# Two of four SBUF-to-SBUF quarter copies moved to the SyncE queue, with the x and B-row loads placed behind their landing

## The chip, the cores and the metric

One Trainium2 chip; the kernel runs on one of its cores. The metric is device time in microseconds from the first to the last instruction of the program with what the runtime adds around it; three runs of the kernel before are given below. All traces are of one execution taken by the hardware profiler.

## What is computed

The reference has two layers over 128 sequences of 32 tokens with 512 features each:

```python
def lora_add(base, inp, A, B):                       # rank 16, one adapter per sequence, picked by index
    t = jnp.einsum('bri,bni->bnr', A[layer_idx][idx], inp)
    return base + jnp.einsum('bor,bnr->bno', B[layer_idx][idx], t) * 0.5
gate = lora_add(x @ W_gate.T, x, A_gate, B_gate)     # 512 -> 1376
up   = lora_add(x @ W_up.T,   x, A_up,   B_up)
act  = silu(gate) * up
down = lora_add(act @ W_down.T, act, A_down, B_down) # 1376 -> 512
x = x + down @ sign(weight).T + bias                 # layer 0
# layer 1: an adapter pair per sequence (64 adapters), then a 512x512 layer with 8 weighted LoRA terms
x = x + ffn(((x @ B1[idx1].T) @ A1[idx1].T))
```

The inputs are float32. The prologue folds the second matrices of both layers into tables, so that the loop has three kinds of products: gate and up (512 to 1376), down (1376 to 512, already multiplied with the signs), and the small adapter products.

## The kernel before

The 4096 tokens are worked through in `G = 32` groups of 128 tokens (four sequences). After a prologue of some 50 us each engine runs `step(g, prev, pp, ...)` for g = 0 to 31, the middle ones in a hardware loop, and then `finish`. The step is a software pipeline over three groups: gate and up of group `g`, down and the layer-0 adapter of group `prev = g - 1`, and layer 1 of group `pp = g - 2`.

The 1376 features are three chunks: chunk 0 of 352 columns, chunks 1 and 2 of 512. Float32 accuracy is had from high and low halves, three matmuls for each block. What the change touches is the way of chunk 2 of the activations from PSUM back to TensorE:

- TensorE ends a step with `second_rows`, which completes gate and up of chunks 1 and 2. In the next step ScalarE applies silu to chunk 1 and chunk 2, VectorE multiplies with up (`gated`) and transposes in 32x32 blocks (`turn_act`, signal `act_turned`: its count for chunk c of group g is `3 g + c + 1`).
- ScalarE then issues `send_act`: for each chunk four DMAs within SBUF, one for each quarter of 32 partitions of `act_sb[c]`, which is spread over the 128 partitions of `landed[c]`. Each of the four adds 16 to `act_in1` or `act_in2`. Before the change ScalarE issues four for chunk 1 and then four for chunk 2, and only then the casts of `split_actT`.
- TensorE meanwhile runs gate and up of chunk 0 and gate and most of up of chunk 1 of the new group. Before the last three matmuls of `up(g, 1)` stands `small_ready`: it waits for both chunks' landings (`act_in1`, `act_in2`), for the adapter rows `ad_in` and for the landed quarters and rows of layer 1. Behind it come the small adapter products (`t_rows`, `td_rows`, `t1_rows`, signal `small_mm`), `down` of chunks 1 and 0, and `first_ready`, which waits for `lhs_ready` (VectorE scales and transposes the small products), for the B rows (`b_in`) and for two more loads. Then `first_rows`, `down` of chunk 2, gate and up of chunk 2, and `second_rows`.
- SyncE issues all loads and stores of a step in one fixed order: x (`load_x`), four B rows (`load_b`), xT and four A rows for the next group (`load_xT` waits for `small_mm`), the copy of `lhs` (`copy_lhs`, waits for `lhs_ready`), four `b1` rows, the store (waits for `out_done`), four pairs of `ad` and `sb` rows, four `c` rows. Where a row is picked by an index, SyncE first loads the index into a register. `load_x` waits before the change for the transpose of chunk 1 (`act_turned` at `3 g + 2`); this also keeps `load_b` from overwriting `b_rows` while `second_rows` reads it.

Lines: `send` L240, `send_act` L245, `load_b` L297, `load_xT` L331, `load_x` L336, `store` L343, `copy_lhs` L347, SyncE's `step` L351, ScalarE's `step` L463, `turn_small` L613, `gate` L794, `up` L807, `down` L819, `small_ready` L864, `first_ready` L893, `first_rows` L901, `second_rows` L913, TensorE's `step` L923. All matmuls of gate and up have line L785.

Of the kernel before, what the change touches and what calls it, by code (L numbers as in the profile page):

```python
# [8 lines left out]
BATCH, SEQ, H = 128, 32, 512  # L9
# [15 lines left out]
NC = len(CHUNKS)  # L25

QUAD = P // 4
SENT = 4 * 16
TURN_W = [3 * P, 4 * P, 4 * P]
# [47 lines left out]
def build_adaln_ffn(nc, xT, x, wgu, signT, wd, bd, btab, atab, adtab, la, lbw, w1T, a1, b1tab, b1end,  # L77
                    bias, ids, consts, sb_table, c_table, out):
    ctx = ExitStack()
    with ctx:  # L80
# [4 lines left out]
        def place(name, shape, dtype, at=None, line=LINE):  # L85
            n = 4 * int(np.prod(shape[1:]))
            n = (n + line - 1) // line * line
            if at is None:
                at = cursor
            t = nc.alloc_sbuf_tensor_at(name, shape, dtype, offset=at[0])  # L90
            at[0] += n
            return t
# [23 lines left out]
        x1_turn = place("x1_turn", [P, H], f32)  # L116
        act_sb = [place(f"act_sb{c}", [P, w], f32) for c, w in enumerate(TURN_W)]
        landed = [place(f"landed{c}", [P, w], f32) for c, w in enumerate(TURN_W)]
        x1_landed = place("x1_landed", [P, H], f32)
# [55 lines left out]
        def sem(name):  # L175
            return ctx.enter_context(nc.semaphore(name))
# [19 lines left out]
        L = {n: sem(n) for n in names}  # L196
# [12 lines left out]
        def last(g):  # L209

            return isinstance(g, int) and g == G - 1
# [12 lines left out]
        def act_in(c):  # L224

            return L[("act_in0", "act_in1", "act_in2")[c]]
# [10 lines left out]

            return slice(b * SEQ, (b + 1) * SEQ)

        def send(engine, to, tile, w, signal):  # L240
            for q in range(4):
                engine.dma_start(to[:, q * w // 4:(q + 1) * w // 4], tile[q * QUAD:(q + 1) * QUAD, 0:w]  # L242
                                 ).then_inc(signal, 16)

        def send_act(engine, g, c):  # L245
            engine.wait_ge(L["act_turned"], g * NC + c + 1)
            send(engine, landed[c], act_sb[c], TURN_W[c], act_in(c))

        def send_x1(engine, g):
            engine.wait_ge(L["x1_turned"], g + 1)  # L250
            send(engine, x1_landed, x1_turn, H, L["x1T_in"])

        def rows_stored(engine):

# [5 lines left out]
        def _(sp):  # L260
# [31 lines left out]
            def load_a(g):  # L292
                for b in range(GB):
                    at = row_of(0, g, b, R0)
                    sp.dma_start(a_raw[:, b, :], atab[bass.ds(at, P), :]).then_inc(L["a_in"], 16)

            def load_b(g):  # L297
                for b in range(GB):
                    at = row_of(0, g, b, R0)
                    sp.dma_start(b_rows[even_rows(0, 4), b, :],  # L300
                                 btab[bass.ds(at, P), :].rearrange("(q r e) w -> q r (e w)", q=4, e=2)
                                 ).then_inc(L["b_in"], 16)

            def load_b1(g):
                for b in range(GB):
                    at = row_of(1, g, b, R1)
                    sp.dma_start(b1_raw[:, b, :], b1tab[bass.ds(at, P), :]).then_inc(L["b1_in"], 16)

            def load_ad_sbd(g):
                if isinstance(g, int) and g < 2:  # L310
                    sp.wait_ge(L["first_mm"], g + 1)
                for b in range(GB):
                    at = row_of(0, g, b, R0)
                    sp.dma_start(ad_raw[:, b, :], adtab[bass.ds(at, P), :]).then_inc(L["ad_in"], 16)
                    sp.dma_start(cs_rows[even_rows(3, 4), b, :], sb_view[bass.ds(at, P), :].rearrange("(r e) w -> r (e w)", e=8)
                                 ).then_inc(L["sbd_in"], 16)

            def load_c(g):
                if last(g):
                    sp.wait_ge(L["first_mm"], g + 2)  # L320
                for b in range(GB):
                    at = row_of(1, g, b, R1)
                    sp.dma_start(cs_rows[even_rows(2, 3), b, :], c_view[bass.ds(at, P), :].rearrange("(r e) w -> r (e w)", e=8)
                                 ).then_inc(L["c_in"], 16)
# [6 lines left out]
            def load_xT(g):  # L331
                after(sp, L["small_mm"], g)
                sp.dma_start(xT_raw[:], xT[bass.ds(g * P, P), :].rearrange("p (k t) -> p k t", k=KC)
                             ).then_inc(L["xT_in"], 16)

            def load_x(g):  # L336
                if last(g):
                    sp.wait_ge(L["x1_done"], g)
                else:
                    sp.wait_ge(L["act_turned"], g * NC + 2)  # L340
                sp.dma_start(x_in[:], x[bass.ds(g * P, P), :]).then_inc(L["x_in"], 16)

            def store(g):  # L343
                sp.wait_ge(L["out_done"], g + 1)
                sp.dma_start(out[bass.ds(g * P, P), :], out_sb[:]).then_inc(L["stored"], 16)

            def copy_lhs(g):  # L347
                sp.wait_ge(L["lhs_ready"], g + 1)
                sp.dma_start(lhs2_sb[2 * QUAD:P, :], lhs_sb[0:2 * QUAD, :]).then_inc(L["lhs2_in"], 16)

            def step(g, prev, pp, nxt):  # L351
                if prev is not None:
                    load_x(prev)
                    load_b(g)
                if nxt is not None:
                    load_xT(nxt)
                    load_a(nxt)
                copy_lhs(g)
                if prev is not None:
                    load_b1(prev)  # L360
                if pp is not None:
                    store(pp)
                load_ad_sbd(g)
                if prev is not None:
                    load_c(prev)

            def finish(g):
                load_x(g)
                sp.wait_ge(L["small_mm"], g + 2)
                for b in range(GB):  # L370
                    at = row_of(1, g, b, R1)
                    sp.dma_start(b1_raw[:, b, :], b1end[bass.ds(at, P), :]).then_inc(L["b1_in"], 16)
                load_c(g)
                store(g - 1)
                sp.wait_ge(L["out_done"], g + 1)
                sp.dma_start(out[g * P:(g + 1) * P, :], x1_turn[:]).then_inc(L["stored"], 16)
                sp.wait_ge(L["stored"], 16 * G)

            sp.wait_ge(S["rows_clear"], 1)
            load_b(0)  # L380
            sp.wait_ge(S["rows_clear"], 2)
            step(0, None, None, 1)
            step(1, 0, None, 2)
            step(2, 1, 0, 3)
            with sp.Fori(3, G - 1) as g:
                step(g, g - 1, g - 2, g + 1)
# [41 lines left out]
        def _(act):  # L428
# [3 lines left out]
            def split_xT(g):  # L432
                act.wait_ge(L["xT_in"], 16 * g + 16)
                for half in range(2):
                    after(act, L["xT_used"], 2 * g - 1 + half)
                    at = slice(2 * half, 2 * half + 2)
                    copy(xT_sb[:, at, 0, :], xT_raw[:, at, :]).then_inc(L["xT_hi"], 1)

            def silu(g, c):
                w = CHUNKS[c][1]  # L440
                act.wait_ge(L["first_mm" if c == 0 else "second_mm"], g + 1)
                after(act, act_in(c), SENT * g)
                nc.scalar.activation(act_sb[c][:, 0:w], gu_ps[GU_BANK[c][0]][:, 0:w], ACT.Silu  # L443
                                     ).then_inc(L["silu_done"], 1)
# [6 lines left out]
            def split_actT(g, c):  # L451
                act.wait_ge(act_in(c), SENT * g + SENT)
                high_actT(c)

            def split_up(c, pieces):

                f, w = CHUNKS[c]
                act.wait_ge(S["down_mm"], BLOCKS_UNTIL[c])
                for k in pieces:
                    act.wait_ge(wu_in[k], 16)  # L460
                    copy(wu_sb[:, 0, k, f:f + w], wu_raw[:, k, f:f + w]).then_inc(S["wu_hi"], 1)

            def step(g, prev, pp, nxt):  # L463
                if prev is not None:
                    silu(prev, 1)
                    silu(prev, 2)
                    send_act(act, prev, 1)
                    send_act(act, prev, 2)
                    split_actT(prev, 1)
                    split_actT(prev, 2)  # L470
                else:
                    split_up(2, range(KC))
                silu(g, 0)
                send_act(act, g, 0)
                if prev is not None:
                    send_x1(act, prev)
                split_actT(g, 0)
                if nxt is not None:
                    split_xT(nxt)
# [663 lines left out]
```

## Time and profile before

| what | us |
|---|---|
| median of three runs | 1050.86 (1047.32 to 1051.44) |
| the profiled execution, its own time | 1048.76 |
| its span, first to last instruction | 1046.4 |
| TensorE matmul busy | 958.4 (92%) |
| TensorE weight load busy | 737.9 (71%) |
| VectorE busy | 430.2 (41%) |
| ScalarE busy | 170.5 (16%) |
| GpSimd busy | 93.5 (9%) |
| mean granted TensorE clock | 0.949 of full |

The profile counts as busy only compute; instructions that issue DMAs are shown as queues (SPq, ACTq), with the time that the engine spends on the issue. The time "to landing" of a DMA runs from the start of its issue to its completion. An idle time with the word "issue" behind it is one for which the profile shows no releaser. The chain of waits is followed back from the last instruction.

### The profile page before, as it was taken

What the parts mean: (1) busy time and instruction counts of PE and PEld (TensorE: products, weight loads), DVE (VectorE), ACT (ScalarE), POOL (GpSimd) and SP (SyncE); (2) the same over time, 40 slices, a digit from 0 to 9 for tenths busy, and PEclk for the clock granted to TensorE, in tenths of its full rate; (3) what the DMA queues carried; (4) which work ended last, traced back from release to release, by engine and by line L of the source; (5) the groups of instructions that cost most, each with busy time, mean ns of one, the idle gap of its engine ahead of it and who ended that gap; (6) DMA issues with size and microseconds to landing.
All of it is one profiled execution on the core that took longest, in us unless ns stands there. A gap on an engine that the chain in (4) does not pass through costs nothing.

```text
span 1046.4 us, 28196 instructions
## 1 busy us (share of the span) xinstructions
PE 958.4 (92%) x10528; PEld 737.9 (71%) x10528; DVE 430.2 (41%) x1051; ACT 170.5 (16%) x318; POOL 93.5 (9%) x81
## 2 busy tenths in 40 slices
PE   9999989999888889988898988898998988899888
PEld 6877767677666767766676766767676667677665
DVE  6753344344333334434343443433444343344433
ACT  6731011111101111110111111111111011111101
POOL 0200000000000000000000000000000000000001
PEclk9999899999999999999999999999999999999989
DMA  9824444453444444344454434444534434453432
GB/s 352 350 69 119 120 115 135 124 138 95 123 122 112 132 128 122 105 129 113 120 132 129 112 108 131 114 123 122 139 107 110 131 107 132 121 139 102 117 94 74
DMA packets 166678, 135.23 MB, mean 129 GB/s; under 512 B 55680, under 2 KB 138368, under 8 KB 166528
## 3 DMA queue, kind: packets, MB, share of 16 engines
q1 hardware_dynamic: 93712, 101.08, 33.5%
q10 hardware_dynamic: 72000, 30.70, 11.1%
q0 software_dynamic: 944, 3.15, 0.8%
q8 instruction: 14, 0.23, 0.1%
q14 instruction: 8, 0.07, 0.0%
HBM read 92.11 MB, written 11.01 MB: 99 GB/s over the span
## 4 chain that ended last, share of the span: by engine, by line
PE 89%; issue 8%; DMA 1%; DVE 1%; ACTq 1%; ACT 0%; SPq 0%
PE gu_ps L785 48%; PE y_ps L829 26%; PE out_ps L849 3%; PE gu_ps L918 3%; PE out_ps L886 2%; PE out_ps L838 2%; PE out_ps L859 1%; PE y_ps L785 1%; PE out_ps L785 1%; PE gu_ps L909 1%; ACTq L242 1%; DMA weff_raw<-in_w1T 1%; DMA landed<-act_sb 0%; PE gu_ps L958 0%; PE y_ps L890 0%
## 5 line engine op out<-in xcount | busy, mean ns | idle before, releaser
L785 PE MATMUL gu_ps<-wu_sb,xT_sb 128*128 128x512 f32 (+1 forms) x1152 | 265.1, 375 | 80.1 <-issue 79.1
L785 PEld LDWEIGHTS gu_ps<-wu_sb,xT_sb 128*128 128x128 f32 x1152 | 205.6, 189 | 120.9 <-issue 93.0
L829 PE MATMUL y_ps<-down_sb,actT_sb 128*128 128x512 f32 x1056 | 273.8, 413 | 0.0
L785 PE MATMUL gu_ps<-wg_sb,xT_sb 128*128 128x512 f32 (+1 forms) x1152 | 255.7, 371 | 0.6 <-DVE xT_sb L576 0.6
L829 PEld LDWEIGHTS y_ps<-down_sb,actT_sb 128*128 128x128 f32 x1056 | 204.8, 200 | 69.6 <-issue 27.3
L785 PEld LDWEIGHTS gu_ps<-wg_sb,xT_sb 128*128 128x128 f32 x1152 | 204.2, 188 | 55.7 <-DVE xT_sb L576 26.7
L576 DVE TENSOR_TENSOR actT_sb<-landed,actT_sb 128x512 fp32r<-128x512 f32 (+1 forms) x96 | 69.9, 728 | 260.4 <-ACT actT_sb L430 259.4
L430 ACT CAST actT_sb<-landed 128x512 fp32r<-128x512 f32 (+1 forms) x96 | 56.3, 586 | 492.1 <-issue 280.3
L596 DVE TENSOR_TENSOR act_sb<-act_sb,gu_ps 128x512 f32<-128x512 f32 (+1 forms) x94 | 58.2, 619 | 122.5 <-ACT act_sb L443 122.5
L619 DVE STREAM_TRANSPOSE lhs_sb<-t_own 32x32 f32<-32x32 f32 x512 | 103.7, 203 | 7.7
L443 ACT ACTIVATE act_sb<-gu_ps 128x512 f32<-128x512 f32 (+1 forms) x96 | 49.8, 553 | 339.4 <-PE gu_ps L909 310.7
L399 POOL TENSOR_TENSOR x_sb<-x_sb,bias_sb 128x512 f32<-128x512 f32 x31 | 39.8, 1284 | 527.4 <-DVE x_turn L632 527.4
L610 DVE TENSOR_TENSOR t_own<-out_ps,const_sb 128x64 f32<-128x64 f32 (+3 forms) x34 | 7.5, 222 | 169.0 <-PE out_ps L859 163.5
L395 POOL TENSOR_TENSOR x_in<-x_in,bias_sb 128x512 f32<-128x512 f32 x32 | 41.3, 1290 | 366.5 <-DMA x_in<-in_x 366.5
L600 DVE STREAM_TRANSPOSE act_sb<-act_sb 128x512 f32<-128x512 f32 (+1 forms) x94 | 62.7, 667 | 3.2
L849 PE MATMUL out_ps<-ad_raw,landed 128*32 128x16 f32 x2816 | 42.2, 211 | 0.0
L849 PEld LDWEIGHTS out_ps<-ad_raw,landed 128*32 128x32 f32 x2816 | 40.1, 151 | 0.2 <-issue 0.2
L918 PE MATMUL gu_ps<-b_rows,lhs_sb 32*32 32x512 f32 x1024 | 36.6, 601 | 0.0
L890 PE MATMUL y_ps<-cs_rows,lhs_sb 32*32 32x512 f32 x256 | 35.8, 600 | 0.0
L886 PE MATMUL out_ps<-cs_rows,lhs_sb 32*32 32x512 f32 x256 | 35.8, 600 | 0.0
L576 DVE TENSOR_TENSOR xT_sb<-xT_raw,xT_sb 128x256 fp32r<-128x256 f32 x64 | 26.7, 422 | 3.4 <-ACT xT_sb L430 0.6
L627 DVE TENSOR_TENSOR x_sb<-x_in,y_ps 128x512 f32<-128x512 f32 x31 | 21.3, 688 | 16.1 <-PE y_ps L829 16.1
(135 smaller groups left out, 441.3 us busy)
## 6 DMA issues: line engine op xcount, KB each, us to landing
b_rows<-in_btab SPq DMA_DIRECT2D x128, 216.0 KB, 3.5
landed<-act_sb ACTq DMA_DIRECT2D x248, 64.0 KB, 2.8
ad_raw<-in_adtab SPq DMA_DIRECT2D x128, 88.0 KB, 2.1
xT_raw<-in_xT SPq DMA_DIRECT2D x32, 256.0 KB, 2.6
a_raw<-in_atab SPq DMA_DIRECT2D x128, 64.0 KB, 1.8
x_in<-in_x SPq DMA_DIRECT2D x32, 256.0 KB, 2.9
x_landed<-x_turn ACTq DMA_DIRECT2D x124, 64.0 KB, 2.3
out_x<-out_sb SPq DMA_DIRECT2D x31, 256.0 KB, 2.1
```

Source lines behind the costliest of these rows:

```text
L395: nc.gpsimd.tensor_tensor(x_in[:], x_in[:], bias_sb[:, 0, :], ALU.add).then_inc(L["x_biased"], 1)
L430: return nc.scalar.copy(o, i)
L443: nc.scalar.activation(act_sb[c][:, 0:w], gu_ps[GU_BANK[c][0]][:, 0:w], ACT.Silu).then_inc(L["silu_done"], 1)
L576: return nc.vector.tensor_tensor(o, whole, hi(high), ALU.subtract)
L596: nc.vector.tensor_tensor(a, a, gu_ps[GU_BANK[c][1]][:, 0:w], ALU.mult).then_inc(L["act_done"], 1)
L600: nc.vector.transpose(act_sb[c][:], act_sb[c][:]).then_inc(L["act_turned"], 1)
L619: turned = nc.vector.transpose(lhs_sb[r * QUAD:(r + 1) * QUAD, tokens(b)], wide[tokens(b), :])
L785: last = nc.tensor.matmul(o, w, m, start=start and n == 0, stop=stop and n == len(terms) - 1, skip_group_check=not check)
L829: last = nc.tensor.matmul(y_ps[:], actT_sb[:, ACTT_SLOT[c] + n, a, :], down_sb[:, blk, b, :], start=c == begin and n == 0 and (a, b) == (0 ...
L849: last = nc.tensor.matmul(small_ps[tokens(b), TD_AT:TD_AT + TD_W], landed[c][:, at:at + SEQ], ad_raw[:, b, blk * RANK:(blk + 1) * RANK], s ...
L886: return nc.tensor.matmul(out_ps[tokens(b), :], lhs_sb[group(2), tokens(b)], cs_rows[group(2), b, :], start=True, stop=True, skip_group_ch ...
L918: last = nc.tensor.matmul(gu_ps[GU_BANK[c][u]][tokens(b), :], lhs[group(r), tokens(b)], b_rows[group(r), b, CHUNKS[0][1]:PAIR], start=Fals ...
```

## The change

SyncE's step issues quarters 0 and 1 of chunk 2 of group `prev`, after the transpose of that chunk; ScalarE issues quarters 2 and 3. `load_x`, and with it everything behind it on SyncE, waits for the landing of all four quarters of chunk 2 instead of the transpose of chunk 1.

```diff
-        def send(engine, to, tile, w, signal):
-            for q in range(4):
+        def send(engine, to, tile, w, signal, quarters):
+            for q in quarters:
                 engine.dma_start(to[:, q * w // 4:(q + 1) * w // 4], tile[q * QUAD:(q + 1) * QUAD, 0:w]
                                  ).then_inc(signal, 16)
 
-        def send_act(engine, g, c):
+        def send_act(engine, g, c, quarters=range(4)):
             engine.wait_ge(L["act_turned"], g * NC + c + 1)
-            send(engine, landed[c], act_sb[c], TURN_W[c], act_in(c))
+            send(engine, landed[c], act_sb[c], TURN_W[c], act_in(c), quarters)
...
@@ load_x (SyncE)
                 if last(g):
                     sp.wait_ge(L["x1_done"], g)
                 else:
-                    sp.wait_ge(L["act_turned"], g * NC + 2)
+                    sp.wait_ge(L["act_in2"], SENT * (g + 1))
                 sp.dma_start(x_in[:], x[bass.ds(g * P, P), :]).then_inc(L["x_in"], 16)
...
@@ step (SyncE)
                 if prev is not None:
+                    send_act(sp, prev, 2, range(0, 2))
                     load_x(prev)
                     load_b(g)
...
@@ step (ScalarE)
                     send_act(act, prev, 1)
-                    send_act(act, prev, 2)
+                    send_act(act, prev, 2, range(2, 4))
                     split_actT(prev, 1)
                     split_actT(prev, 2)
```

## Rows read from the trace of the kernel before

**Rows 1.** The page: shares of the longest chain, and the costliest matmul group with its idle time.
```profile
PE 89%; issue 8%; DMA 1%; DVE 1%; ACTq 1%; ACT 0%; SPq 0%
L785 PE MATMUL gu_ps<-wu_sb,xT_sb 128*128 128x512 f32 (+1 forms) x1152 | 265.1, 375 | 80.1 <-issue 79.1
```
**Rows 2.** Waits (engine, line, releaser: us in total, times, longest): TensorE's at 80 to 90 us, then SyncE's at 170 to 990 us.
```profile
PE gu_ps L785 <- DMA landed<-act_sb: 1.0, 1, 1.0
...
SPq L333 <- PE out_ps L859: 142.1, 27, 6.4
SPq L345 <- DVE out_sb L644: 10.6, 20, 1.0
```
**Rows 3.** Timeline of TensorE (start, duration, what, idle before): first, second, middle and last stall.
```profile
112.86 0.95 PE L785 MATMUL gu_ps<-wu_sb,xT_sb 128*128 128x512 f32 x3 [2.10 <-issue]
...
145.44 0.96 PE L785 MATMUL gu_ps<-wu_sb,xT_sb 128*128 128x512 f32 x3 [2.66 <-issue]
...
531.01 1.14 PE L918 MATMUL gu_ps<-b_rows,lhs_sb 32*32 32x512 f32 x32
...
543.01 1.06 PE L785 MATMUL gu_ps<-wu_sb,xT_sb 128*128 128x512 f32 x3 [2.03 <-issue]
...
1003.22 0.93 PE L785 MATMUL gu_ps<-wu_sb,xT_sb 128*128 128x512 f32 x3 [2.51 <-issue]
```
**Rows 4.** Windows: length, busy of PE, PEld, DVE, ACT, POOL; granted clock, DMA share, GB/s.
```profile
84.30:86.30 2.00, 1.94 (x123) 1.57 (x123) 0.00 (x0) 0.46 (x1) 0.00 (x0) 1.00 0.00 0
...
145.44:147.83 2.39, 2.37 (x155) 1.89 (x156) 0.00 (x0) 0.26 (x1) 0.00 (x0) 1.00 0.03 7
147.83:152.80 4.97, 4.97 (x27) 3.87 (x29) 4.16 (x18) 0.00 (x0) 0.00 (x0) 1.00 0.34 94
152.80:172.20 19.40, 19.36 (x146) 14.84 (x145) 7.13 (x13) 3.41 (x7) 1.55 (x2) 1.00 0.47 122
540.98:543.01 2.03, 0.00 (x1) 0.01 (x1) 0.90 (x1) 0.37 (x1) 0.35 (x1) 1.00 0.98 298
543.01:546.20 3.19, 3.19 (x156) 2.64 (x156) 0.00 (x0) 0.26 (x1) 0.00 (x0) 0.61 0.14 54
546.20:551.58 5.38, 5.38 (x25) 4.17 (x21) 4.16 (x18) 0.00 (x0) 0.00 (x0) 0.91 0.36 98
551.58:570.99 19.41, 19.41 (x146) 14.86 (x145) 7.44 (x13) 3.41 (x7) 2.57 (x2) 1.00 0.49 127
```
**Rows 5.** Timeline of VectorE and ScalarE: last transpose, all eight sends, the fifth on, the last.
```profile
535.10 0.71 DVE L600 STREAM_TRANSPOSE act_sb<-act_sb 128x512 f32<-128x512 f32 x1
...
534.52 5.39 ACTq L242 DMA_DIRECT2D landed<-act_sb  x8
...
537.22 1.21 ACTq L242 DMA_DIRECT2D landed<-act_sb  x2
537.79 1.46 ACTq L242 DMA_DIRECT2D landed<-act_sb  x2
...
539.28 0.62 ACTq L242 DMA_DIRECT2D landed<-act_sb  x1
```
**Rows 6.** DMA issues, us to landing: sends starting 536.42, 538.45 and 539.28, each alone.
```profile
landed<-act_sb ACTq DMA_DIRECT2D x1, 64.0 KB, 2.2
landed<-act_sb ACTq DMA_DIRECT2D x1, 64.0 KB, 3.9
landed<-act_sb ACTq DMA_DIRECT2D x1, 64.0 KB, 3.3
```
**Rows 7.** Timeline of SyncE's queue from one xT load to the next; last B row apart.
```profile
516.90 0.34 SPq L333 DMA_DIRECT2D xT_raw<-in_xT  x1
517.95 3.06 SPq L295 DMA_DIRECT2D a_raw<-in_atab  x4
521.06 0.52 SPq L349 DMA_DIRECT2D lhs_sb<-lhs_sb  x1
...
536.87 0.33 SPq L341 DMA_DIRECT2D x_in<-in_x  x1
537.78 3.88 SPq L300 DMA_DIRECT2D b_rows<-in_btab  x4
546.47 0.34 SPq L333 DMA_DIRECT2D xT_raw<-in_xT  x1
...
541.19 0.47 SPq L300 DMA_DIRECT2D b_rows<-in_btab  x1
```
**Rows 8.** One tile's DMAs, us from issue to landing, min, median, max: landed, then b_rows (500 to 562 us).
```profile
DMA to landing us min/median/max: 2.0/2.5/4.0
...
DMA to landing us min/median/max: 3.0/3.4/3.7
```

More of the change, by code:

```diff
@@ L238, in tokens @@
             return slice(b * SEQ, (b + 1) * SEQ)
-        def send(engine, to, tile, w, signal):
-            for q in range(4):
+        def send(engine, to, tile, w, signal, quarters):
+            for q in quarters:
                 engine.dma_start(to[:, q * w // 4:(q + 1) * w // 4], tile[q * QUAD:(q + 1) * QUAD, 0:w]
                                  ).then_inc(signal, 16)
-        def send_act(engine, g, c):
+        def send_act(engine, g, c, quarters=range(4)):
             engine.wait_ge(L["act_turned"], g * NC + c + 1)
-            send(engine, landed[c], act_sb[c], TURN_W[c], act_in(c))
+            send(engine, landed[c], act_sb[c], TURN_W[c], act_in(c), quarters)
         def send_x1(engine, g):
             engine.wait_ge(L["x1_turned"], g + 1)
-            send(engine, x1_landed, x1_turn, H, L["x1T_in"])
+            send(engine, x1_landed, x1_turn, H, L["x1T_in"], range(4))
         def rows_stored(engine):
```

## Prediction

> **What bounds the kernel now.** I read the page first: TensorE holds 89% of the chain that ended last and "issue" another 8%; nearly all of the latter is one place, 79.1 us of idle time before matmuls of gate and up, L785 [rows 1]. The reader is to see that this is no spread-out loss. The timeline of TensorE shows it as one stall in each step, always before the three matmuls that stand behind `small_ready`: thirty stalls of 2.0 to 3.3 us, from 112.86 to 1003.22, and a shorter one of 1.0 us in step 1 [rows 2, 3]. So 29 periods fill 1003.22 - 112.86 = 890.4 us, 30.70 us each. What `small_ready` waits for is told by ScalarE's queue: eight sends take 5.39 us from 534.52 on, the last starts at 539.28 and lands 3.3 us later, at 542.6; TensorE goes on at 543.01 [rows 3, 5, 6]. The fourth send (536.42) landed in 2.2 us, before SyncE's x load (536.87) and B rows were on the way, the seventh and eighth needed 3.9 and 3.3 us [rows 6, 7], with the DMA engines at 0.98 of their time in the stall [rows 4]. The change goes at both halves of this delay: the queueing on ScalarE and the shared DMA engines.
>
> The stall has a second cost. Behind it TensorE's granted clock drops from 1.00, that is 2.4 GHz, to half, 1.2 GHz, for a stretch: 0.61 and 0.91 in the two windows after 543.01. In step 3 the clock stayed at 1.00 although the stall was 2.66 us; from the three matmuls to `first_rows` that took 2.39 + 4.97 = 7.4 us, against 3.19 + 5.38 = 8.6 with the drop [rows 4]. The remaining 19.4 us of a step are the same in both. So TensorE's own work is 26.7 us a step at full clock, 28.0 with the drop: 30.70 is 28.0 and a stall of 2.7.
>
> **The change part by part.** Let T be the end of `second_rows`, 531.01 + 1.14 = 532.15 in the step shown [rows 3]. TensorE reaches `small_ready` at T + 8.8 (540.98).
>
> *ScalarE's sends.* It now issues six instead of eight. The sixth started at 537.79, T + 5.6, instead of the eighth at T + 7.1 [rows 5]. Nothing else of its own is moved; its cast of chunk 1 comes up to 1.4 us earlier, which no one waits for.
>
> *The landing of chunk 2.* With x and B rows held back, a quarter should land in 2.2 us (the fourth send's value, which I take, since it too had only other sends beside it); bounds 2.0 and 4.0 from all sends [rows 6, 8]. ScalarE's half is there at T + 7.8, 1.0 before TensorE asks. It costs nothing up to a landing of 3.2.
>
> *SyncE's own circle.* This is the dear part. From xT (516.90) to x (536.87) SyncE needs 19.97 us of issuing; from x to the end of the fourth B row (541.66) 4.79; and from there to xT at least 0.05 (the gap behind the A rows before `copy_lhs`, the nearest row) [rows 7]. That is 24.8 us of work, and the rest of the period is its wait for `small_mm` at xT, 142.1 us in 27 steps, 5.3 each [rows 2]. The change adds, before x: two sends, the second 0.65 after the first (eight in 5.39 us), its landing 2.2, and waking up with the register work for x, 0.15, an estimate that lies below the 0.4 TensorE took from the landing (542.6) to 543.01. That is 3.0, so SyncE can't go round in under 27.8 us. Bounds: 0.57 + 2.0 gives 27.4 (and 27.2 if the B rows issue faster without ScalarE's beside them); 0.83 (538.45 to 539.28) + 3.3 + 0.4 gives 29.3 [rows 6]. Its wait of 5.3 us is what pays for this, and it goes nearly whole. In this state SyncE comes to the sends later than the transpose (535.81, T + 3.7), so that the wait for the transpose costs nothing, and TensorE may wait some tenths for SyncE's half.
>
> *The B rows.* They now start behind the landing. x at T + 8.0, the fourth B row 4.32 later (541.19 - 536.87), landed after 3.0 to 3.4 [rows 7, 8], at T + 15.3 to 15.7. TensorE wants them before the last three matmuls of `down(prev, 0)`: after 8.8 + 7.4 - 0.8, T + 15.4 at full clock, T + 16.6 with the drop. From there to the next T it needs some 11.6 us (three matmuls 0.75, `first_rows` to `second_rows` 10.6, and 0.3 to start again). This circle thus lasts 26.9 to 27.3, up to 28.4 with the slowest landings. The rows had more than a microsecond of cover before, and now have none at full clock.
>
> *What moves with it.* xT, the A rows, the copy of `lhs`, the `b1` rows, the store, the `ad` and `sb` rows and the `c` rows all stand behind the wait. In the new period xT is issued some 1.5 us later against TensorE than now; all of them are wanted in the next step, or, as the copy of `lhs`, 8 us after its issue. The x load is wanted only by GpSimd and by VectorE's sum after `down(prev, 2)`, 12 us on. I cost them at nothing.
>
> A rule that speaks against the half of the change that shares the sends: the Trainium skill, "DMA: Bandwidth & Descriptors", sections "Issuing engines are not separate DMA queues" and "Rules for kernel authors", says that DMAs from several engines run on the same 16 DMA engines and that this saves only issue time. The rows agree that sharing the engines costs landing time (2.2 against 3.9). By the rule the split would be worth just the two sends' issue, T + 7.1 to T + 5.6. The gate alone would then give a landing at T + 9.3, a stall of 0.5 to 0.8 and a period near 28.5, an estimate; with the split the sum stays as worked out here.
>
> **The sum.** The period is the largest of three: TensorE 26.7 or 28.0, SyncE 27.8, B rows 27. If the clock stays up, SyncE sets 27.8 and TensorE stalls 1.1 us a step; if it still drops, TensorE sets 28.0 nearly without a stall. In step 1, with a stall of 1.0, it stayed at 1.00 [rows 2, 4]. Both ends lie so near that I take 28.0. Then 29 x (30.70 - 28.0) = 78.3, and about 2 more from the stalls of step 1 and 2 (1.0 and 2.1, half of each kept): 80. The tail is untouched: step 31 has no xT and no A rows to issue, and the last x load waits for `x1_done` as before. The profiled execution's 1048.8 becomes 968.5; the median of the runs lies 2.1 above that execution, so 970.
>
> **Rivals.**
>
> 1. *Forecast*, period 27.7 to 28.4: 958 to 979. Chance 0.52.
> 2. *SyncE's circle is longer* than I count, because sends from two engines at once issue in 0.83 and land in 3.3, or the B rows are late in addition: period 28.4 to 29.3, 980 to 1006. For it: 24.8 of the 27.8 are measured, but the 3.0 comes from ScalarE's rows. Chance 0.24.
> 3. *The circles overlap better*: the clock stays full and both circles fall to 27.2: 29 x 3.5 + 3 = 104, 946; up to 957. Against it: it needs the lower bounds all at once. Chance 0.17.
> 4. *Slower.* The B rows take the stall's place at `first_ready`. With the slowest landings, sends 4.0 and B rows about 4.2 by estimate (0.8 over the median), the circle is 5.6 + 4.0 + 0.15 + 4.3 + 4.2 + 11.6 = 29.9; the clock would then drop in dense matmuls, 3.4 us at half speed (two windows: 0.39 of 3.19 and 0.09 of 5.38 us lost, doubled), costing up to 1.7: 31.6, 29 x 0.9 = 26 us slower, 1077. It decides from a period over 30.7, a circle without clock loss of over 29. Against it: the sends land alone. Chance 0.04.
> 5. *The change does not do what it says*: SyncE comes so late to its two quarters that they land no earlier than the eighth send did (T + 10.4). It would need SyncE free only at T + 7.6; before it was free at 536.87, T + 4.7. Time 1050. Chance 0.03.
>
> **How the numbers follow.** 970 is the forecast of case 1. The range takes cases 1 and most of 2 and 3: 950 to 1002. A change below 0.5% (5 us) can't be told from none here. Faster by over 0.5% is cases 1 to 3 and a little of the next: 0.93; within 0.5%: 0.03; slower 0.04.
>
> **What would show it.** Right: the idle time before L785 falls from 79 to under 35 us; SyncE's wait for `small_mm` at L333 falls from 5.3 to about nothing in a step and a wait for the landing of about 2 us stands before x; the sends land in about 2.2; the xT loads follow each other at 27.8 to 28.2 us. Wrong: xT loads at over 29 us or under 27.5; a stall before L829 or L886 that is larger than the old one; a landing of over 3 us of sends that nothing accompanies. Should the clock still drop in every step with no stall before it, TensorE's 28.0 was the bound and not SyncE.

## The result and the profile after

| | before | after |
|---|---|---|
| median, us | 1051.15 | 962.34 (960.8 to 964.34) |
| ratio to before | | 0.9167, 95% interval 0.9135 to 0.92 |
| span of the profiled execution | 1046.4 | 959.9 |
| mean granted TensorE clock | 0.949 | 0.998 |

The change makes the kernel 8.3% faster. The median before is of four runs, one of them a slow outlier of 1488.36 us; without it the median is 1050.86, and the ratio leaves it out. The first line below is the page's chain by engine, the others its costliest groups with idle time (line, engine, what, count, then busy, mean ns of one, then idle before it). Lines below `send_act` have moved down by one: gate and up are L786, down is L830.

```profile
PE 95%; issue 3%; DMA 1%; DVE 0%; ACT 0%; ACTq 0%; SPq 0%
...
L830 PE MATMUL y_ps<-down_sb,actT_sb 128*128 128x512 f32 x1056 | 267.1, 401 | 13.8 <-issue 13.7
L786 PE MATMUL gu_ps<-wu_sb,xT_sb 128*128 128x512 f32 (+1 forms) x1152 | 256.6, 369 | 7.1 <-issue 7.1
```

The idle time at gate and up went from 80 us to 7 [rows 1]; 14 us of a new idle time stand before down. The stall has become small and has in part moved from `small_ready` to `first_ready`. The waits of SyncE's queue at 170 to 900 us (line, releaser: us in total, times, longest) tell what it waits for now:

```profile
SPq L341 <- DMA landed<-act_sb: 37.0, 26, 1.5
```

That is the only one. The wait for `small_mm` at xT, 5.3 us in each step before [rows 2], is gone, and so is that for the store; SyncE now waits 1.4 us in each step for the landing, and for nothing else. Its own timeline, from xT load to xT load (start, duration, what), to be laid beside [rows 7]:

```profile
504.58 0.34 SPq L333 DMA_DIRECT2D xT_raw<-in_xT  x1
...
524.16 1.37 SPq L242 DMA_DIRECT2D landed<-act_sb  x2
527.23 0.34 SPq L341 DMA_DIRECT2D x_in<-in_x  x1
528.15 3.77 SPq L300 DMA_DIRECT2D b_rows<-in_btab  x4
532.30 0.34 SPq L333 DMA_DIRECT2D xT_raw<-in_xT  x1
```

This is a closed circle of 27.72 us: 19.58 from xT to the first send, 3.07 from there over the landing to x, 4.69 to the end of the B rows, 0.38 to xT. The 26 xT periods from 171.6 to 893.2 us have a mean of 27.76. TensorE in the same step shows what it has left over. The first row is the three matmuls behind `small_ready`, as in [rows 3]; the other two are `down` of chunks 1 and 0, cut by the wait for the B rows before its last three matmuls:

```profile
527.42 0.96 PE L786 MATMUL gu_ps<-wu_sb,xT_sb 128*128 128x512 f32 x3 [0.27 <-issue]
...
529.89 4.36 PE L830 MATMUL y_ps<-down_sb,actT_sb 128*128 128x512 f32 x18
534.86 0.94 PE L830 MATMUL y_ps<-down_sb,actT_sb 128*128 128x512 f32 x3 [0.61 <-issue]
```

These are two stalls, of 0.27 and 0.61 us. The windows over this step (columns as in [rows 4]) are at full clock throughout:

```profile
527.42:529.89 2.47, 2.47 (x156) 2.02 (x156) 0.00 (x0) 0.26 (x1) 0.00 (x0) 1.00 0.49 140
529.89:535.73 5.84, 5.23 (x25) 3.75 (x22) 4.17 (x18) 0.00 (x0) 1.29 (x1) 1.00 0.68 204
535.73:555.10 19.37, 19.37 (x147) 15.01 (x147) 7.76 (x13) 3.89 (x8) 1.28 (x1) 1.00 0.42 112
```

The quarters of all three chunks land in 1.9, 2.2 and 3.2 us (min, median, max at 170 to 900 us), against 2.0, 2.4 and 4.6 before. These figures hide most of the effect, since they count the quarters of chunks 0 and 1 in. The four quarters of chunk 2 alone, over the same time, went from a median of 3.6 us to 2.2, and their last landing from T + 11.1 to T + 8.6, in the mean of the steps. T is the end of `second_rows`, as in the prediction.

### The profile page after: what moved, and what is told of

Its sections match the earlier page's. It is cut to its first block, busy times and chain, and to the rows that moved or that the text cites. A ratio compares the mean times of both kernels' runs of the same rounds, so it can differ in the third digit from the quotient of the medians.

```text
span 959.9 us, 28224 instructions
## 1 busy us (share of the span) xinstructions
PE 928.4 (97%) x10528; PEld 708.2 (74%) x10528; DVE 422.8 (44%) x1051; ACT 170.2 (18%) x318; POOL 93.2 (10%) x81
## 4 chain that ended last, share of the span: by engine, by line
PE 95%; issue 3%; DMA 1%; DVE 0%; ACT 0%; ACTq 0%; SPq 0%
PE gu_ps L786 52%; PE y_ps L830 27%; PE gu_ps L919 3%; PE out_ps L850 3%; PE out_ps L887 2%; PE y_ps L786 1%; PE out_ps L839 1%; PE out_ps L786 1%; PE gu_ps L910 1%; PE out_ps L860 1%; PE gu_ps L959 0%; DMA landed<-act_sb 0%; DMA lb_raw<-in_lbw 0%; PE gu_ps L1031 0%; ACTq L242 0%
## 5 line engine op out<-in xcount | busy, mean ns | idle before, releaser
L830 PE MATMUL y_ps<-down_sb,actT_sb 128*128 128x512 f32 x1056 | 267.1, 401 | 13.8 <-issue 13.7
L786 PE MATMUL gu_ps<-wu_sb,xT_sb 128*128 128x512 f32 (+1 forms) x1152 | 256.6, 369 | 7.1 <-issue 7.1
L830 PEld LDWEIGHTS y_ps<-down_sb,actT_sb 128*128 128x128 f32 x1056 | 192.0, 189 | 89.8 <-issue 39.8
L786 PE MATMUL gu_ps<-wg_sb,xT_sb 128*128 128x512 f32 (+1 forms) x1152 | 256.0, 371 | 1.5 <-DVE xT_sb L577 1.5
L786 PEld LDWEIGHTS gu_ps<-wg_sb,xT_sb 128*128 128x128 f32 x1152 | 204.3, 188 | 56.9 <-DVE xT_sb L577 27.8
L786 PEld LDWEIGHTS gu_ps<-wu_sb,xT_sb 128*128 128x128 f32 x1152 | 204.7, 188 | 44.0 <-issue 16.1
L577 DVE TENSOR_TENSOR actT_sb<-landed,actT_sb 128x512 fp32r<-128x512 f32 (+1 forms) x96 | 62.2, 648 | 221.9 <-ACT actT_sb L431 220.9
L850 PE MATMUL out_ps<-ad_raw,landed 128*32 128x16 f32 x2816 | 34.1, 186 | 0.0
L850 PEld LDWEIGHTS out_ps<-ad_raw,landed 128*32 128x32 f32 x2816 | 31.5, 108 | 0.5 <-issue 0.2
L577 DVE TENSOR_TENSOR xT_sb<-xT_raw,xT_sb 128x256 fp32r<-128x256 f32 x64 | 26.6, 421 | 4.6 <-ACT xT_sb L431 3.8
```

The source lines that it names most:

```text
L577: return nc.vector.tensor_tensor(o, whole, hi(high), ALU.subtract)
L786: last = nc.tensor.matmul(o, w, m, start=start and n == 0, stop=stop and n == len(terms) - 1, skip_group_check=not check)
L830: last = nc.tensor.matmul(y_ps[:], actT_sb[:, ACTT_SLOT[c] + n, a, :], down_sb[:, blk, b, :], start=c == begin and n == 0 and (a, b) == (0 ...
L850: last = nc.tensor.matmul(small_ps[tokens(b), TD_AT:TD_AT + TD_W], landed[c][:, at:at + SEQ], ad_raw[:, b, blk * RANK:(blk + 1) * RANK], s ...
```

## The experiments

Three theories are tested:

- Theory A: in the changed kernel SyncE's own circle of issues sets the period, not TensorE and not the B rows' landing.
- Theory B: the sharing of the sends carries the gain and the place of the loads does little.
- Theory C: the place of the loads behind the landing (the gate, below) carries it.

All edits are made to the changed kernel. The ratio is that to the kernel before, timed on the same chip; the period from xT to xT is the mean at 170 to 900 us of one trace.

| kernel | median us | ratio, 95% interval | us from xT to xT |
|---|---|---|---|
| changed | 962.3 | 0.9167 (0.9135 to 0.92) | 27.76 |
| loads behind the landing, sends not shared | 983.7 | 0.9393 (0.9334 to 0.9452) | 28.40 |
| sends shared, loads not behind the landing | 939.5 | 0.8957 (0.8902 to 0.9012) | 26.81 |
| neither, x behind the transpose of chunk 2 | 1049.2 | 0.999 (0.9973 to 1.0008) | 30.29 |
| changed, one more issue on SyncE | 981.3 | 0.9352 (0.9294 to 0.941) | 28.42 |
| changed, four more issues | 1024.6 | 0.9772 (0.973 to 0.9814) | 29.81 |
| changed, B rows before x | 959.7 | 0.9149 (0.9092 to 0.9205) | 27.77 |
| changed, x issued by GpSimd | 946.0 | 0.8998 (0.8963 to 0.9033) | 27.26 |
| changed, x before the landing | 944.8 | 0.8993 (0.8961 to 0.9025) | 27.19 |
| sends shared, B rows not behind the landing, x by GpSimd | 927.3 | 0.8833 (0.8801 to 0.8866) | 26.59 |

### Each half of the change alone

```diff
@@ gate only: SyncE's step
-                    send_act(sp, prev, 2, range(0, 2))
@@ ScalarE's step
-                    send_act(act, prev, 2, range(2, 4))
+                    send_act(act, prev, 2)
```

> The changed kernel, but ScalarE sends all four quarters of chunk 2 (x and the B rows stay behind their landing). Theory A (SyncE's circle of issues bounds the changed kernel, 27.7 us a step): here SyncE has two sends less, its circle is no bound; the eighth send leaves at T + 7.1 and lands alone at T + 9.3, so TensorE stalls 0.5 to 0.8 us at small_ready, the B rows come 1.4 us later, and the period is 28.0 to 28.5: 970 to 985 us. Theory B (the sharing of the sends carries the gain, the place of the loads little): stall of 2 us or more and the clock drop stay, over 1020. Theory C (the gate alone carries it): 962, as the changed kernel.

Measured: 983.7 us, period 28.40. Rows of TensorE, ScalarE and SyncE's x load (start, duration, what), with the end of `second_rows` at 528.42 + 1.15 = 529.57 as T:

```profile
528.42 1.15 PE L918 MATMUL gu_ps<-b_rows,lhs_sb 32*32 32x512 f32 x32
...
539.26 0.96 PE L785 MATMUL gu_ps<-wu_sb,xT_sb 128*128 128x512 f32 x3 [0.86 <-issue]
...
531.93 5.43 ACTq L242 DMA_DIRECT2D landed<-act_sb  x8
...
538.90 0.62 ACT L430 CAST actT_sb<-landed 128x512 fp32r<-128x512 f32 x1 [0.82 <-DMA landed<-act_sb]
...
539.07 0.33 SPq L341 DMA_DIRECT2D x_in<-in_x  x1
```

The cast starts at the landing, T + 9.3, as theory A had it; TensorE has stalled 0.86 here, and 0.7 in the mean (17.4 us in 26 stalls). It waits almost as much for the B rows before `down`, 16.0 us in 26. Theories B and C are out as stated: the gate alone gives three quarters of the changed kernel's gain (65 of 89 us, each against the kernel before on its own chip), and the rest needs the sharing.

```diff
@@ split only: load_x
-                    sp.wait_ge(L["act_in2"], SENT * (g + 1))
+                    sp.wait_ge(L["act_turned"], g * NC + 3)
```

> The changed kernel, but x waits only for the transpose of chunk 2, not for the landing; the sends stay shared. Theory A: SyncE's circle loses the 2.4 us between its second send and x, to about 25.5 of issue, and waits for small_mm again; the loads run beside ScalarE's last two sends, which then land in 3 to 3.9 instead of 2.2, at T + 8.6 to 9.5, a stall of 0 to 0.8 us: period 26.9 to 27.6, 940 to 960 us. Theory C (without the gate the contention brings the stall back): stall of 1.5 to 2.5 and the clock drop again, 985 to 1030. If landing is what counts and SyncE's circle nothing: slower than the changed kernel by the added stall.

Measured: 939.5 us, period 26.81, just under the range of theory A, and faster than the changed kernel by more than either interval. SyncE's queue, and what ScalarE waits for:

```profile
514.47 1.34 SPq L242 DMA_DIRECT2D landed<-act_sb  x2
516.02 0.44 SPq L341 DMA_DIRECT2D x_in<-in_x  x1
517.05 3.79 SPq L300 DMA_DIRECT2D b_rows<-in_btab  x4
...
512.33 3.85 ACTq L242 DMA_DIRECT2D landed<-act_sb  x6
...
518.64 0.62 ACT L431 CAST actT_sb<-landed 128x512 fp32r<-128x512 f32 x1 [1.61 <-DMA landed<-act_sb]
```

From its first send to x SyncE needs 1.55 us instead of 3.07. It waits for `small_mm` again (12.1 us in 23 waits), so its circle is no bound. And the contention that the gate should keep away is small: both queues' sends have left by 516.2, just as x starts, and the last has landed by 518.64. It isn't nothing: the last quarter of chunk 2 lands in 2.9 us here (median at 170 to 900 us), against 2.2 in the changed kernel and 4.1 before. Once the sends are shared, the loads leave behind them by the order on the queue alone. In the kernel before, x and the B rows left beside the fifth to the eighth send [rows 5, 7].

So the sharing does two things at once. In the mean of the steps the last send leaves at T + 5.6 instead of T + 7.1, and x at T + 6.1 instead of T + 4.7. The last landing of chunk 2 comes 2.75 us earlier than before (T + 8.37 against T + 11.12): 1.45 of it is the earlier send, the rest the shorter landing. No run has one of these without the other. The two halves of the change are then two remedies for one stall, and beside the sharing the gate costs more than it brings: it lengthens SyncE's circle.

The control for this run: it also moves x from behind the transpose of chunk 1 to that of chunk 2.

```diff
-                    sp.wait_ge(L["act_in2"], SENT * (g + 1))
+                    sp.wait_ge(L["act_turned"], g * NC + 3)
-                    send_act(sp, prev, 2, range(0, 2))
-                    send_act(act, prev, 2, range(2, 4))
+                    send_act(act, prev, 2)
```

> A control: the kernel before, with x waiting for the transpose of chunk 2 instead of chunk 1; ScalarE sends all eight quarters. Theory A: SyncE reached x at T + 4.7 already, behind that transpose at T + 3.7, so nothing changes: within 4 us of the kernel before, the stall of 2.7 us and the clock drop stay. It shows whether the later signal alone, without the sharing, explains the run in which only the sends were shared. Rival (x and B rows starting a little later let the eighth send land sooner): 5 to 20 us faster.

Measured: 1049.2 us, ratio 0.999. The later signal does nothing by itself; x leaves at T + 4.7 as before. The period of 30.29 is from one of the two quickest of its twelve runs, 1041.4 us.

### Is SyncE's circle the bound?

```diff
@@ SyncE's step
                 load_ad_sbd(g)
                 if prev is not None:
+                    after(sp, L["spare_in"], 16 * prev)
+                    sp.dma_start(spare[:], consts[:, 0:16]).then_inc(L["spare_in"], 16)
                     load_c(prev)
```

> The changed kernel with one more small load (8 KB, needed by nobody) on SyncE in each step, ahead of the c rows. Theory A: SyncE's circle is the bound, so each step grows by the whole issue, 0.5 to 0.7 us: 15 to 21 us slower, 977 to 983. Rival (the circle through the B rows' landing or TensorE's own work is the bound): within 3 us of the changed kernel.

Measured: 981.3 us, 18.9 more; the period is 28.42, 0.66 more. A load that no one needs is paid for in each step, although TensorE was 97% busy by the page of the changed kernel.

```diff
@@ SyncE's step; the wait for act_in2 stands in load_b too
-                    load_x(prev)
-                    load_b(g)
+                    load_b(g)
+                    load_x(prev)
```

> The changed kernel with the four B rows ahead of the x load, both behind the landing. Theory A: SyncE's circle has the same instructions, so the time stays within 3 us of the changed kernel; the B rows land some 0.9 us earlier and the idle time in front of down's last three matmuls goes, and comes back in front of gate and up at small_ready. Rival (the circle from landing over B rows and first_rows to the next landing is the bound): 0.5 to 0.9 us a step less, 15 to 26 us faster.

Measured: 959.7 us, with an interval that holds the changed kernel's ratio, and the same period of 27.77. TensorE's waits at 170 to 900 us, of the changed kernel and then of this one:

```profile
PE y_ps L830 <- issue: 13.5, 24, 1.0
PE gu_ps L786 <- issue: 5.7, 14, 0.5
```

```profile
PE gu_ps L788 <- issue: 12.3, 25, 0.8
PE y_ps L832 <- issue: 5.4, 17, 0.9
```

The idle time moves from down to gate and up, and its sum stays, 19.2 against 17.7. The B rows' landing decides where TensorE waits, not how long the step is.

```diff
@@ SyncE: no load_x in step and finish, load_b waits for act_in2; GpSimd:
+            def load_x(g):
+                if not last(g):
+                    pool.wait_ge(L["act_in2"], SENT * (g + 1))
+                pool.dma_start(x_in[:], x[bass.ds(g * P, P), :]).then_inc(L["x_in"], 16)
             with pool.Fori(1, G - 1) as g:
+                load_x(g)
                 add_bias0(g)
```

> The changed kernel with the x load issued by GpSimd's queue, behind the same landing; SyncE's B rows wait for the landing themselves. Theory A: SyncE's circle loses x's 0.9 us, 27.75 to about 26.85, close to TensorE's own 26.7 and to the circle through the B rows, which start 0.9 earlier: period 26.9 to 27.2, 938 to 948 us. Rival (SyncE's circle is not the bound): within 3 us of the changed kernel.

Measured: 946.0 us, inside what was expected, but with a period of 27.26, just above it. The queue shows why the 0.92 us from x to the first B row (528.15 - 527.23 in the changed kernel) did not go whole:

```profile
517.73 1.52 SPq L242 DMA_DIRECT2D landed<-act_sb  x2
521.32 3.70 SPq L302 DMA_DIRECT2D b_rows<-in_btab  x4
...
545.03 1.33 SPq L242 DMA_DIRECT2D landed<-act_sb  x2
```

From the first send to the first B row it takes 3.59 us, against 3.07 + 0.92 = 3.99 in the changed kernel. The landing still comes 2.9 after the first send in both (mean of the steps). Behind it x left after 0.2, and the first B row leaves after 0.6; by the code a row index is loaded in between. The circle is closed, 545.03 - 517.73 = 27.30, and SyncE waits for nothing but the landing.

```diff
@@ load_x waits for act_turned (g * NC + 3); load_b for act_in2
```

> The changed kernel with x issued right after SyncE's two sends (waiting for the transpose), and only the B rows behind the landing. Theory A: x's 0.9 us of issue lies in the wait for the landing, which costs SyncE nothing then, unless x stretches the landing of the last quarters beside it: period 26.8 to 27.2, 936 to 948 us. Rival (contention with x counts): landing 0.3 to 0.7 longer, period 27.3 to 27.7, 950 to 962.

Measured: 944.8 us, period 27.19. Putting x into the wait is worth as much as taking it off the queue. Its contention with the sends costs nothing that is seen: the quarters of chunk 2 have a median landing of 2.2 us here as in the changed kernel.

```diff
@@ load_b waits for act_turned (3 g); x on GpSimd's queue behind act_in2, as above
```

> The kernel with the sends shared and the B rows behind the transpose only, and in addition x on GpSimd's queue behind the landing. Theory A: TensorE's own 26.7 us a step is the bound already (26.8 with x on SyncE), so this brings at most 0.1 a step: 936 to 940 us. Rival (SyncE's or the DMA engines' load still costs): 5 us or more below the shared-sends run of 939.5.

Measured: 927.3 us, 12 below the run with shared sends, where I had expected at most 3 or 4: theory A's figure missed, and the rival's "5 us or more" is what came. This is the fastest version, 3.6% below the changed kernel. Here TensorE sets the time almost alone. Its timeline over the place of the old stall:

```profile
719.22 2.93 PE L794 MATMUL gu_ps<-wg_sb,xT_sb 128*128 128x512 f32 x12
721.99 2.88 PE L794 MATMUL gu_ps<-wu_sb,xT_sb 128*128 128x512 f32 x12
724.80 0.46 PE L847 MATMUL out_ps<-a_raw,xT_raw 128*32 128x32 f32 x32
```

The twelve matmuls of up run through, and nearly every step takes 26.55 to 26.68 us. That is TensorE's own work at full clock.

With x on SyncE's queue about half of the steps are 26.6 and the others 26.8 to 27.5. There x leaves beside the last send, the last quarter lands in 2.9 us instead of 2.2, and `small_ready` waits 0.2 to 0.6 us in nine steps. The steps are 0.2 longer in the mean, 6 us of the 12. Most of the rest lies in step 2, step 3 and the last, which were 3.2, 1.5 and 3.4 us longer in the one trace. In step 2 and the last, TensorE stands still among the small matmuls of layer 1, for 2.15 and 2.57 us against 0.76 and 1.09 in the fastest version, and behind both of these longer stalls the clock drops. In step 3 it is a stall of 1.37 us at `small_ready`. The windows over them, with shared sends and then in the fastest version, have the granted clock third from the right:

```profile
112.00:122.00 10.00, 7.85 (x173) 6.47 (x173) 4.16 (x18) 0.00 (x0) 0.00 (x0) 0.83 0.37 103
896.00:906.00 10.00, 7.43 (x98) 5.73 (x96) 4.16 (x18) 0.00 (x0) 0.00 (x0) 0.83 0.15 49
```

```profile
110.00:120.00 10.00, 9.24 (x201) 7.22 (x214) 4.84 (x19) 0.62 (x1) 1.84 (x2) 1.00 0.56 172
885.00:895.00 10.00, 8.91 (x156) 6.49 (x145) 5.31 (x21) 0.47 (x1) 1.28 (x1) 1.00 0.23 72
```

What these small matmuls wait for the trace does not tell, and it was not tried.

### The clock

```diff
@@ the same as one more issue, with four
+                    for n in range(4):
+                        sp.dma_start(spare[:, n, :], consts[:, 0:16]).then_inc(L["spare_in"], 16)
```

> The changed kernel with four more small loads (8 KB each, needed by nobody) on SyncE in each step, ahead of the c rows; one such load cost 0.66 us a step. Theory A (SyncE's circle is the bound, whatever the clock): period 27.76 + 0.66 + 3 x 0.53 to 0.66, that is 30.0 to 30.4, 1026 to 1040 us, near the kernel before. It also asks about the clock: if a long stall at small_ready is what brings the drop of the granted clock, TensorE's idle time of some 3.5 us a step, parted between small_ready and the B rows, brings it back where one part passes 2 us (mean clock 0.95); if the drop belonged to the small matmuls alone it would have been in the changed kernel too, which shows 0.998.

Measured: 1024.6 us, 1.4 below the range that I gave, since the further loads cost 0.47 us each and not 0.53. The period is 29.81, again without a wait of SyncE other than for the landing. The mean clock is 0.974, between before and after, and above the 0.95 that I had expected. Windows behind three stalls of this trace, of 1.52, 2.46 and 1.81 us:

```profile
351.51:354.51 3.00, 3.00 (x157) 2.46 (x158) 0.41 (x2) 0.26 (x1) 0.50 (x1) 1.00 0.50 154
...
411.26:414.26 3.00, 3.00 (x153) 2.49 (x155) 0.00 (x0) 0.26 (x1) 0.59 (x1) 0.62 0.50 155
...
441.03:444.03 3.00, 3.00 (x156) 2.55 (x156) 0.05 (x1) 0.25 (x1) 0.60 (x1) 0.77 0.53 159
```

Over its 28 steps from 142 to 948 us: behind 9 stalls of 0.83 to 1.57 us the clock never fell below 1.00; behind 14 of 1.68 to 2.10 us it fell to half, 1.2 GHz, in 8; behind 5 of 2.46 to 2.63 us in all. So the clock does follow the stall at `small_ready`: the longer it is, the more often the clock falls. The length alone does not decide it. In the kernel before, the stall of 2.66 us in step 3 had no drop behind it, and in the control run four of 31 stalls had none, the longest 2.89 us, while one of 1.76 us had. The small matmuls are the same in all kernels here and do not bring the drop alone.

## Why the prediction was right, and where it was off

The forecast was 970, the range 950 to 1002, and 962.3 was measured.

- **One stall and its clock drop make up the loss.** Right. Between the first `second_rows` and the last, before and after differ by 950.8 - 864.2 = 86.6 us, the whole of the difference of the spans (86.5); prologue and tail are the same to 0.2 us. TensorE's own 26.7 us at full clock was read off step 3 alone; in the fastest version it is 26.6.
- **SyncE's circle, 27.8 us.** Right: 27.72 in the step shown, 27.76 in the mean. By its terms: 19.97 was 19.58, as the store no longer waits; 4.79 was 4.69; the gap before xT was 0.38, not 0.05; from the first send over the landing to x it was 3.07, not 3.0. The prediction's own rows had shown that something was missing: 24.8 of work and 5.3 of wait are 30.1, and the period was 30.7. One more issue showed that this circle is the bound.
- **The step that was off is the last of the sum.** I took 28.0 for the period because I left open whether the clock would still drop, and TensorE would need 28.0 then. It held (0.998): TensorE's work was 1.1 us below the period, of which 0.7 is seen as stalls, and SyncE's 27.8 stood. That is 29 x 0.24 = 7 us of the 8 us of the miss. The trace of before had one stall of 1.0 us at full clock to go by; the clock experiment has nine below 1.6. The forecast was near since the two ends, 27.8 and 28.0, lay so close, and not because the choice between them was right.
- **Two slips in the working** had no effect on the forecast. By its own sum periods of 27.7 to 28.4 are 962 to 982 us, and not 958 to 979. And the B rows' circle "up to 28.4 with the slowest landings" can't be had from the rows: with 3.9 for the send and 3.7 for the B row its terms add up to 29.3.
- **The landing of 2.2 us.** Right in size, but only half understood. I credited it to the gate. In the run with the sends shared and no gate the quarters of chunk 2 have a median of 2.2 as well, and the last one 2.9. The prediction counted the gate's 2.4 us on SyncE's circle and never asked what the kernel would be without it, though the same sum gives 25.5 for that circle. Beside the sharing the gate is a net loss of 23 us.
- **The B rows.** Their circle, 26.9 to 27.3 by the estimate, was rightly no bound, though the idle time before down, 14 us, is theirs; exchanging x and B rows moved it and gained nothing.
- **What moves with it costs nothing.** Right: no wait of TensorE, VectorE or SyncE on any of these loads is new.
- **The estimate for the gate alone**, T + 9.3 and a period near 28.5, was met: T + 9.3 and 28.40. Its stall of 0.5 to 0.8 was 0.7 in the mean.
- **The worth of the split.** By the rule quoted there (the Trainium skill, "DMA: Bandwidth & Descriptors", section "Issuing engines are not separate DMA queues"), sharing DMAs among engines saves only the time of their issue. In this case's traces ScalarE's last send does leave 1.45 us earlier with the sends shared. But on one queue the sends also hold back the loads behind them, which the rule doesn't speak of, and the last quarter's landing went from 4.1 us to 2.9. Together the two were worth 109 us; no run prices them apart.
- **The slower rival** (stall moved to `first_ready`, over dense matmuls, with a clock drop) did not come about: the stalls there, up to 1.0 us, left the clock at 1.00.

## What to carry to other kernels

A queue that issues loads all the time has a budget of time for each step, as a compute engine has. When a wait is put on it, add up its whole circle (all issues, the register loads, the new wait) and compare it with the bound's period; here nearly half of 5.3 us of slack was spent on a gate whose work the order on the queue already did for the most part. Where a stall has two causes, price each remedy alone before taking both. Work that needs no wait, as x here, belongs before the wait's end or on an idle queue.

## What the runs showed of the hardware

- In the run with four extra issues the granted clock stayed at full behind 9 of 9 stalls of TensorE of up to 1.57 us; it fell to half behind 8 of 14 of 1.68 to 2.10 us, and behind 5 of 5 above 2.4 us. In the kernel before, with 2.0 to 3.3 us, it fell in all but one of thirty steps, the one with 2.66 us. A drop costs 1.2 us of work in its step (8.57 against 7.36 us) on top of the stall.
- A 64 KB copy within SBUF lands in 2.2 us, whichever of the two queues issues it, and in 3.6 (median of the quarters of chunk 2 before, at most 4.6) when x and B rows (1.1 MB) run beside it.
- An 8 KB load costs its queue 0.66 us when alone in its place, and 0.47 when it follows its like.
- Taking a DMA out from behind a wait saved less than its own time, since the next one has a register to load: 0.40 us of 0.92.
